# Expert weights of two mixtures: read from a DRAM table over the partitions instead of spread by a matmul

## What is computed

```python
def mixture0(x):                    # 1024 tokens, 16 experts, 4 of them chosen, in 2 of 4 groups
    scores = sigmoid(x @ router.T)
    tidx = topk(masked_by_group(scores + e_bias), 4)
    tw = scores[tidx] / (sum(scores[tidx]) + 1e-20) * 2.5
    h = silu(einsum('th,eih->tei', x, gate_w)) * einsum('th,eih->tei', x, up_w)      # i = 64
    yo = einsum('tei,ehi->teh', h, down_w)
    combine = zeros((T, 16)).at[token, tidx].add(tw)
    return einsum('te,teh->th', combine, yo) + shared_mlp(x)
# mixture3 is the same with 64 experts, 6 chosen in 4 of 8 groups, scores that include the bias,
# 1e-8 in the denominator and no factor 2.5
x = x + tanh(g_xattn[0]) * attention0(layernorm(x), ctx)
x = x + tanh(g_ffn[0]) * mixture0(layernorm(x))
...
x = x + tanh(g_ffn[3]) * mixture3(layernorm(x))
```

## Time and profile before

| | us |
|---|---|
| three plain runs | 698.71, 701.78, 708.68; median 701.78 |
| profiled execution | 699.08, of which the span is 697.3 |
| TensorE busy | 636.2 (91%) |
| VectorE busy | 419.7 (60%) |
| ScalarE busy | 377.8 (54%) |
| GpSimd busy | 195.4 (28%) |

### The profile page before, as it was taken

One profiled execution on the slowest core, in us unless ns is written; L12 is line 12 of the kernel. 1 busy time (PEld: TensorE's weight loads), 2 busy tenths in 40 slices (PEclk: granted clock), 3 DMA queues, 4 the chain that ended last, 5 costly groups with the idle time before them and its releaser, 6 DMA issues.

```text
span 697.3 us, 11157 instructions
## 1 busy us (share of the span) xinstructions
PE 636.2 (91%) x3615; PEld 440.7 (63%) x3618; DVE 419.7 (60%) x822; ACT 377.8 (54%) x663; POOL 195.4 (28%) x192
## 2 busy tenths in 40 slices
PE   6999987899699998999988999899996799999997
PEld 3457764675554446999953444467764577777885
DVE  2078839757732447777525565378839655656565
ACT  3567764455445334555554443577864356565553
POOL 4000024472010000000000244000023377777775
PEclk9999978999789999999999999999978999999999
DMA  8100002010000000000000000100001021121210
GB/s 298 44 1 3 1 1 76 1 47 0 1 0 1 0 1 0 1 1 0 1 1 0 24 23 16 46 2 1 2 17 60 1 61 51 55 49 56 60 31 31
DMA packets 9610, 18.55 MB, mean 27 GB/s; under 512 B 1856, under 2 KB 3024, under 8 KB 9440
## 3 DMA queue, kind: packets, MB, share of 16 engines
q1 hardware_dynamic: 9568, 18.01, 8.4%
HBM read 17.48 MB, written 0.52 MB: 26 GB/s over the span
## 4 chain that ended last, share of the span: by engine, by line
PE 79%; DVE 11%; ACT 5%; issue 3%; POOL 1%; DMA 1%; another core or an unknown queue 0%; DVEq 0%; ACTq 0%; SPq 0%; POOLq 0%
PE bank L676 7%; PE bank L678 7%; PE bank L677 7%; PE bank L593 4%; PE bank L926 4%; PE bank L913 4%; PE bank L604 4%; PE bank L485 3%; PE bank L619 3%; PE bank L522 2%; PE bank L690 2%; PE bank L534 2%; PE bank L1011 2%; PE bank L551 2%; PE bank L890 2%
## 5 line engine op out<-in xcount | busy, mean ns | idle before, releaser
L394 POOL TENSOR_TENSOR h_lo<-wc,h_hi 128x512 fp32r<-128x512 f32 x82 | 106.0, 1293 | 69.8 <-ACT h_hi L1200 68.6
L1609 DVE TENSOR_TENSOR wb<-wa,bank 128x512 f32<-128x512 f32 x80 | 55.0, 687 | 69.9 <-PE bank L678 64.3
L1192 ACT ACTIVATE wa<-bank 128x512 f32<-128x512 f32 x84 | 50.4, 600 | 75.5 <-PE bank L678 75.3
L1414 DVE TENSOR_REDUCE row_max<-bank 128x4 f32<-128x512 f32 (+1 forms) x96 | 65.7, 685 | 34.3 <-PE bank L593 19.4
L1127 ACT ACTIVATE wb<-wa 128x512 f32<-128x512 f32 x96 | 60.2, 629 | 33.7 <-DVE wa L1418 33.3
L676 PE MATMUL bank<-xn_hi,w_hi 128*128 128x512 f32 x168 | 68.8, 410 | 8.0 <-DVE wc L1613 3.7
L1418 DVE TENSOR_TENSOR wa<-bank,row_max 128x512 f32<-128x512 f32 x96 | 66.4, 691 | 9.9 <-ACT wb L1127 4.4
L1133 ACT ACTIVATE wc<-bank 128x512 f32<-128x512 f32 x96 | 57.0, 594 | 23.6 <-PE bank L551 15.2
L678 PE MATMUL bank<-xn_hi,w_lo 128*128 128x512 f32 x168 | 66.9, 398 | 0.0
L677 PE MATMUL bank<-xn_lo,w_hi 128*128 128x512 f32 x168 | 66.9, 398 | 0.0
L1200 ACT ACTIVATE h_hi<-wc 128x512 fp32r<-128x512 f32 x84 | 52.4, 624 | 16.1 <-DVE wc L1613 10.0
(11 more groups left out here) (271 smaller groups left out, 1260.4 us busy)
## 6 DMA issues: line engine op xcount, KB each, us to landing
ring<-in_experts SPq DMA_DIRECT2D x42, 256.0 KB, 2.6
ring<-in_experts SPq DMA_DIRECT2D x8, 192.0 KB, 2.4
mats<-in_mats SPq DMA_DIRECT2D x1, 1472.0 KB, 9.8
mats<-in_mats SPq DMA_DIRECT2D x1, 832.0 KB, 6.0
mats<-in_mats SPq DMA_DIRECT2D x2, 320.0 KB, 8.1
x<-in_x_t SPq DMA_DIRECT2D x1, 512.0 KB, 4.2
context<-in_ctx_t SPq DMA_DIRECT2D x1, 512.0 KB, 4.8
select<-in_select SPq DMA_DIRECT2D x1, 512.0 KB, 11.0
```

The source lines that it names most:

```text
L394: nc.gpsimd.tensor_tensor(h_lo[:, k % 2, :], wc[:, k % 2, :], h_hi[:, k % 2, :].bitcast(f32), ALU.subtract).then_inc(m_h_lo, 1)
L1414: v.tensor_reduce(row_max[:, u % 2, 0:heads], s, X, ALU.max).then_inc(a_max, 1)
L1609: v.tensor_tensor(wb[:, par, :], wa[:, par, :], bank[2 + par][:, :], ALU.mult)\
```

## The change

`split_weights`, the matmul `weight` and its semaphore `m_weight` are gone, and so is the use of the fourth 128 columns of each pair: loads and ScalarE's split cover 384 columns. `route_weights` writes the weights whole. After the transposition ScalarE copies only the 16 or 64 rows that carry experts. SyncE then (`half`) stores these rows of one half of the tokens to a table in DRAM, waits for the store, and for each of the four slots issues two loads (`pair_weights`), each of which reads one row of the table 64 times, into the upper or lower 64 partitions of `pair_w`, in the free region of `arena`. For later rounds the loads take all 1024 tokens at once, after the last `wc` that uses the slot, ahead of the load of the next pair's weights in the same queue. `wc` reads `pair_w` instead of a PSUM bank and waits for the slot's loads. The loop over rounds in SyncE's program is written out. Apart from the mixtures, VectorE fills 128 columns with ones at the start and TensorE multiplies them eleven times (`keep_busy`) before the first layer norm.

```diff
@@ -64,6 +64,7 @@
         q_rows = arena[:, 12288:16384].rearrange("p (g t) -> p g t", g=QUADS)
+        idle_w = arena[:, 512:512 + P]
...
@@ -106,7 +107,10 @@
         comb_pieces = sb("comb_pieces", [P, 8, P])
-        comb_t = sb("comb_t", [P, T], f32r)
+        comb_t = sb("comb_t", [P, T])
+        pair_w = arena[:, 8192:12288].rearrange("p (s t) -> p s t", s=4)
+        comb_rows = [nc.dram_tensor(f"comb_rows{n}", (e, T), f32).ap() for n, e in enumerate((16, 64))]
...
@@ -196,11 +200,13 @@
         m_shift = signal("m_shift")
-        m_g, m_u, m_cb, m_silu, m_t, m_h, m_h_hi, m_h_lo, m_down = (
-            signal(n) for n in ("m_gate", "m_up", "m_weight", "m_silu", "m_prod", "m_hidden", "m_hidden_hi",
+        m_g, m_u, m_silu, m_t, m_h, m_h_hi, m_h_lo, m_down = (
+            signal(n) for n in ("m_gate", "m_up", "m_silu", "m_prod", "m_hidden", "m_hidden_hi",
         m_x_lo = [signal("m_x_lo0"), signal("m_x_lo1")]
+        m_rows = signal("m_rows")
+        pair_in = [signal(f"pair_in{s}") for s in range(4)]
...
@@ -219,6 +225,8 @@
             m["q0"] = MOE[0]["pairs"] + 1 if n else 0
+            m["w0"] = 64 + 32 * (MOE[0]["rounds"] - 1) if n else 0
...
@@ -314,22 +322,46 @@
             def fill(m, q):
-                sp.dma_start(ring[:, (q + 3) % 4, :], m["weights"][q]).then_inc(w_in[(q + 3) % 4], 16)
+                sp.dma_start(ring[:, (q + 3) % 4, 0:384], m["weights"][q, :, 0:384]).then_inc(w_in[(q + 3) % 4], 16)
+            def pair_weights(m, q, slot, tokens):
+                for j in range(2):
+                    row = comb_rows[m["n"]][2 * q + j:2 * q + j + 1, tokens]
+                    sp.dma_start(pair_w[64 * j:64 * j + 64, slot, tokens],
+                                 row.to_broadcast([64, tokens.stop - tokens.start])).then_inc(pair_in[slot], 16)
-                with sp.Fori(1, m["rounds"]) as i:
-                    for j in range(4):
-                        slot = (j + 3) % 4
-                        sp.wait_ge(m_w_lo, m["q0"] + 4 * i + j - 3)
-                        sp.dma_start(ring[:, slot, :], m["weights"][ds(4 * i + j, 1), :, :].squeeze(0))\
-                            .then_inc(w_in[slot], 16)
-                sp.wait_ge(m_w_lo, m["q0"] + m["pairs"] - 3)
-                fill(m, m["pairs"])
+                n, u0, q0 = m["n"], m["u0"], m["q0"]
+                def refill(q):
+                    sp.wait_ge(m_w_lo, q0 + q - 3)
+                    fill(m, q)
+                def half(c):
+                    tokens = slice(c * HALF, c * HALF + HALF)
+                    sp.wait_ge(m_combE, 4 * n + c + 1)
+                    sp.dma_start(comb_rows[n][:, tokens], comb_t[0:m["E"], tokens]).then_inc(m_rows, 16)
+                    sp.wait_ge(m_rows, 16 * (2 * n + c + 1))
+                    for slot in range(4):
+                        pair_weights(m, slot, slot, tokens)
+                refill(4)
+                half(0)
+                refill(5)
+                refill(6)
+                half(1)
+                for i in range(1, m["rounds"]):
+                    last_use = FIRST_LAST_USE if i == 1 else LAST_USE
+                    for slot in range(4):
+                        sp.wait_ge(m_h, u0 + 2 + 8 * (i - 1) + last_use[slot] + 1)
+                        pair_weights(m, 4 * i + slot, slot, slice(0, T))
+                        if 4 * i + slot + 3 <= m["pairs"]:
+                            refill(4 * i + slot + 3)
...
@@ -465,6 +497,11 @@
+            def keep_busy(n, to):
+                for _ in range(n):
+                    mm(to[:, 0:P], idle_w, idle_w, start=True, stop=True)
...
@@ -685,11 +722,6 @@
-                def weight(slot, c, k):
-                    mm(bank[4 + k % 2][:, :], w_hi[:, slot, 384:512], comb_t[:, c * HALF:c * HALF + HALF],
-                       start=True, stop=True).then_inc(m_cb, 1)
...
@@ -698,8 +730,6 @@
                     pe.wait_ge(m_comb, 4 * n + c + 1)
-                    if c == 1:
-                        pe.wait_ge(m_h, u0 + 4)
...
@@ -714,8 +744,6 @@
                             combine_t(1)
-                            pe.wait_ge(m_combE, 4 * n + 2)
-                        weight(slot, c, k)
...
@@ -729,15 +757,14 @@
                 gate_up(*FIRST_ORDER[1], 1, u0 + 3, q0 + 1 + FIRST_ORDER[1][0], True)
-                pe.wait_ge(m_combE, 4 * n + 1)
-                for k in range(2):
-                    weight(*FIRST_ORDER[k], k)
-            pe.wait_ge(prepared, 3)
+            pe.wait_ge(prepared, 1)
+            keep_busy(11, bank[7])
+            pe.wait_ge(prepared, 4)
...
@@ -1177,7 +1204,7 @@
                         act.wait_ge(m_down, used)
-                    fn(w_hi[:, slot, :], ring[:, slot, :], ACT.Copy).then_inc(m_w_hi, 1)
+                    fn(w_hi[:, slot, 0:384], ring[:, slot, 0:384], ACT.Copy).then_inc(m_w_hi, 1)
...
@@ -1202,7 +1229,8 @@
                     act.wait_ge(m_combT, 4 * n + c + 1)
-                    fn(comb_t[:, c * HALF:c * HALF + HALF], bank[4 + c][:, :], ACT.Copy)\
+                    rows = slice(0, m["E"])
+                    fn(comb_t[rows, c * HALF:c * HALF + HALF], bank[4 + c][rows, :], ACT.Copy)\
...
@@ -1508,12 +1536,6 @@
                 return rt[:, n, 0:4 * e].rearrange("p (t e) -> p t e", t=4)
-            def split_weights(comb, e, c):
-                dst = comb_pieces[:, BH * c:BH * c + BH, :]
-                link(v.tensor_copy(dst[:, :, 0:e].bitcast(f32r), comb))
-                return v.tensor_tensor(dst[:, :, e:2 * e].bitcast(f32r), comb, dst[:, :, 0:e], ALU.subtract)
...
@@ -1591,15 +1613,18 @@
                 link(v.reciprocal(total, total))
-                link(v.tensor_tensor(picked, picked, total.unsqueeze(2).to_broadcast([P, 4, E]), ALU.mult))
+                share = total.unsqueeze(2).to_broadcast([P, 4, E])
+                pieces = comb_pieces[:, BH * c:BH * c + BH, 0:E]
                 if n == 0:
-                    link(v.tensor_scalar(picked, picked, 2.5, None, ALU.mult))
-                split_weights(picked, E, c).then_inc(m_comb, 1)
+                    link(v.tensor_tensor(picked, picked, share, ALU.mult))
+                    v.tensor_scalar(pieces, picked, 2.5, None, ALU.mult).then_inc(m_comb, 1)
+                else:
+                    v.tensor_tensor(pieces, picked, share, ALU.mult).then_inc(m_comb, 1)
-                def products(k, unit, weighed, older):
+                def products(k, unit, weighed, older, i=0):
...
@@ -1609,8 +1634,11 @@
                         dve.wait_ge(m_t, unit - 2 * n - 1)
-                        dve.wait_ge(m_cb, unit - 2 * n - 1)
-                        v.tensor_tensor(wc[:, par, :], wb[:, par, :], bank[4 + par][:, :], ALU.mult)\
+                        first = isinstance(i, int) and i == 0
+                        slot, c = (FIRST_ORDER if first else ORDER)[k]
+                        dve.wait_ge(pair_in[slot], m["w0"] + (32 * (c + 1) if first else 64 + 32 * i))
+                        v.tensor_tensor(wc[:, par, :], wb[:, par, :], pair_w[:, slot, c * HALF:c * HALF + HALF],
+                                        ALU.mult)\
...
@@ -1630,12 +1658,12 @@
                 route_weights(m, 1)
-                products(0, u0 + 4, True, True)
-                products(1, u0 + 5, True, True)
+                products(2, u0 + 4, True, True)
+                products(3, u0 + 5, True, True)
                     for k in range(4 if first else 0, 8):
-                        products(k, u0 + 2 + 8 * i + k, True, True)
+                        products(k, u0 + 2 + 8 * i + k, True, True, i)
...
@@ -1649,6 +1677,7 @@
+            v.memset(idle_w, 1.0).then_inc(prepared, 1)
...
@@ -1660,7 +1689,7 @@
             dve.wait_ge(a_bias, 1)
-            dve.wait_ge(prepared, 4)
+            dve.wait_ge(prepared, 5)
```

## The result

The changed kernel takes 718.56 us in the median (715.45 to 723.7, four runs) against 703.04 (four runs) beside it: a ratio of 1.022, 95% interval 1.012 to 1.033. It is slower, as forecast; whether by more than 2% these four runs leave open. The executions of a kernel fall into a quicker and a slower group, and ratios and intervals here are taken from the quicker one, medians from all. The profiled execution of the changed kernel took 715.45 us, with a span of 713.7 against 697.3.

The account below looks back on a forecast made before the run. TensorE bounds the mixtures' long middle (2.31 us a unit), waits the openings. From the profiled 699.1 us, +19.4 (loops), +7 (table) and -1 (warm-up) give 724.5, called 724; range 698 to 748.

Parts of the forecast that it names:

- The mechanism: Mixture loops: `wc`, now with two SBUF inputs, and GpSimd's instructions exclude each other; the second stands, then needs 0.55 or 1.17 us.
- Rival 1: Mixture loops: TensorE stays the bound, no engine stands, `wc` lasts 0.7 us; 688.5 us in all; chance 0.10.
- Rival 2: Mixture loops: VectorE and GpSimd pack well, 2.17 to 2.4 us a unit, 695 to 712 us; chance 0.17.
- rival 3: Mixture loops: GpSimd's queue goes ahead of a waiting `wc`, 2.7 to 3.06 us a unit, 733 to 759 us; chance 0.12.
- Rival 4: Mixtures' first rounds: the table is the cost, its loads landing near 8 us, 747 us in all; chance 0.04.
- loops of both mixtures, ends included: 72 units at 2.58 us instead of 2.31, the removed matmul included: +19.4 us.
- openings (table): Openings of both mixtures: the weights' way through DRAM delays the first `wc` of a half; +7 us, bounds +4 and +30.
- start: Before the first layer norm: eleven warm-up matmuls speed up the first four centring matmuls; -1 us, at best 1.9 gained.
- the simple cycle of 2.58: Mixture loops: GpSimd's `h_lo` always first, `wc` ends 0.55 us behind it; 2.58 us a unit, the pace taken.
- the walk that gave 2.52: Mixture loops: four units walked with `h_lo` and `w_lo`, a waiting VectorE served first; 10.1 us, 2.52 each.
- the 4.8 of the sum: Mixture openings: from ScalarE's copy to the first `wc`, store 2.0, issue 0.4 and load 2.4 us, together 4.8.
- The 1.6 us that I had added: Mixture openings: TensorE's clock falls while it waits; seven matmuls at twice their time, 1.6 us in both mixtures together.

Follow-up runs that it names:

- before_sbuf: Kernel before, with `wc` reading layer norm's output in SBUF instead of the PSUM bank, tenth matmul kept, no table, tokens' weights left out: 722.16 us, ratio 1.029.
- fix_psum: Changed kernel with the first product written in place into the up product's PSUM bank, where `wc` reads it: 695.96 us, ratio 0.991; measured again 693.85 us, 0.987.
- after_short_h: Changed kernel with GpSimd's `h_lo` cut from 512 to 64 tokens, the rest zeros filled once in each opening: 683.89 us in one run.
- no_table: Changed kernel without the table's store, loads and waits; `wc` multiplies by the layer norm's output in SBUF, tokens' weights left out: 711.29 us in one run.
- fix_short_w2: fix_psum with GpSimd's `w_lo` cut from 384 to 64 columns, the rest zeros filled once in each opening: 690.71 us in one run.
- fix_no_warm_b: fix_psum without the eleven matmuls at the start, measured beside fix_psum: 700.24 us, ratio 0.991 to the kernel before.

## Why the prediction was right, and where not

**The mechanism** was right, and it is shown: by before_sbuf (the operand alone makes the loss), fix_psum (moved back, the loss is gone with all else kept) and after_short_h (GpSimd's side shortened, gone as well). The Trainium skill ("SBUF — State Buffer", "Who interferes with whom") says that a VectorE instruction with two SBUF inputs contends with a GpSimd one that reads SBUF, that the shared access is an exclusive lock, and that the order of issue decides who blocks; the traces agree, with 0.54 us from GpSimd's end to VectorE's here, and 0.55 in the earlier trace rows.

**Rival 1** (TensorE stays the bound, 688.5) fell: it needed `wc` at 0.69 us. That it had a sound sum is seen in after_short_h, where `wc` is 0.70: 682.1. **Rival 2** (2.17 to 2.4 a unit) and **rival 3** (2.7 to 3.06) lie on either side of the 2.549. **Rival 4** had a load landing near 8 us; the 128 KB loads land in 3.0.

**The terms of the sum**, against the two profiled executions:

| term | forecast | measured |
|---|---|---|
| loops of both mixtures, ends included | +19.4 | +14.6 (12.5 + 0.8 + 0.7 + 0.6) |
| openings (table) | +7 | +6.7 (3.0 + 3.7) |
| start | -1 | -5.1 |
| stages between, behind | 0 | +0.2 |
| sum | +25.4 | +16.4 |

The loop was over-sized. I had 2.58 against 2.31, a difference of 0.27; measured were 2.549 against 2.337, that is 0.212. The step that failed is half in each. The 2.31 was the pace of the quiet middle alone, while behind the first round one unit takes 3.43 us in both kernels (560.03 to 563.46 before, 562.32 to 565.76 after): there TensorE waits for the next pair's `w_lo`, and the change adds nothing. And of the walks, the simple cycle of 2.58, in which GpSimd always comes first, is not what runs: 44 of 80 `wc` stood, and units alternate, as in the walk that gave 2.52, some with `wc` behind `h_lo` (1.69 us), some with `h_lo` behind `wc` (1.74). The measured pace lies between the two.

The openings came out near the forecast, 6.7 for 7. ScalarE's copies of the weights' rows in the changed kernel:

```profile
112.22 0.59 ACT L1233 ACTIVATE comb_t<-bank 16x512 f32<-16x512 f32 x1 [2.71 <-PE bank L734]
...
125.42 0.59 ACT L1233 ACTIVATE comb_t<-bank 16x512 f32<-16x512 f32 x1 [1.28 <-PE bank L734]
...
534.81 0.59 ACT L1233 ACTIVATE comb_t<-bank 64x512 f32<-64x512 f32 x1 [3.52 <-PE bank L734]
...
549.18 0.59 ACT L1233 ACTIVATE comb_t<-bank 64x512 f32<-64x512 f32 x1 [1.76 <-PE bank L734]
```

From the end of a copy to the `wc` that waits for it pass 5.3, 5.3, 5.7 and 6.2 us, not the 4.8 of the sum. Against that, the first copy of each mixture ends 0.5 and 0.8 us earlier behind the first gate matmul than before, not 0.2 and 0.3. So the first `wc` comes 2.4 and 2.5 us later there (forecast 2.2 and 2.0), and the fifth, the first of the second half, 3.7 and 3.0 (forecast 3.2 and 2.0): the second half of mixture 2 was not hidden, VectorE waits 2.93 us for its loads. The granted clock up to the fifth `wc` is 0.87 in mixture 1 where it was 0.94, and 0.85 in mixture 2 where it was 0.83. The 1.6 us that I had added for it are about what the waits were short by. Without any weights to wait for (no_table) the fifth `wc` of mixture 2 comes 27.6 us behind the first gate matmul, against 30.9 before and 33.9 with the table: about half of the wait in the changed kernel was there before.

The start was under-sized: I bounded it by the four matmuls of the earlier trace rows, which are 1.7 us shorter but over only 1.4 us earlier, since the eleven are not "over well before" x lands but end 0.5 us behind it; and the profiles have 2 to 5 us there. Since the forecast was 724 and the profiled execution 715.45, these two terms are the whole miss of some 9 us: 4.8 from the loop, 4.1 from the start.

Of the signs I had named, TensorE "about 80% busy" needs a word: the page shows 90%, because matmul records overlap the wait of the next one; counted by issue, 350 times 0.231 in 99.70 us, it is 81%.

## What to carry over

Before an operand moves from PSUM to SBUF, write down for that instruction and for all that run beside it on the other engine where every operand lies, and look in the trace for a pair of the new kind: the two such rows gave the loops' loss to within 5 us, where the removed matmul alone promised a gain of 16.6. If the place must change, keep the other operand in PSUM; here one product written in place turned 2% slower into 1% faster. A transfer that replaces a matmul early in a stage is paid in latency: here the openings grew by 6.7 us, with four waits of 2.0 to 3.5 us in them. The steps that it relieves are worth counting as carefully as the ones it adds.

## What the runs showed of the hardware that I had not expected

**The table's way in the changed kernel.** SyncE's rows at the opening of mixture 2 (start, us, queue, line):

```profile
535.42 0.47 SPq L348 DMA_DIRECT2D comb_rows<-comb_t  x1
537.68 4.94 SPq L334 DMA_DIRECT2D arena<-comb_rows  x8
```

The store is waited for 2.26 us from its issue. Each of the eight loads, which spread one row over 64 partitions, takes 0.6 us to issue, not the 0.42 of the earlier trace rows, so the last pair's load is issued some 4.9 us behind the store's landing. The weights' own loads land in 3.9 us instead of 2.4, and no wait for them is among the changed kernel's waits in the mixtures.

**`w_lo` as the second.** Behind a `wc` of 0.69 us it takes another 0.89 us (after_short_h), where `h_lo` needs 1.12 to 1.15 more and `wc` 0.54: most of the own work of each still lies ahead when the other ends.

**The clock of a stage that no edit touches.** The stages between the mixtures take 357.8 to 363.0 us in eight profiled executions, but 368.5 to 371.1 in four (fix_short_w2, before_sbuf, fix_no_warm_b and fix_psum_b). The last is the same kernel as fix_psum, and its profiled execution, 704.32 us, was the longest of its six. The two from 440 to 480 us, first fix_psum, then fix_psum_b (us, busy us of PE, PEld, DVE, ACT, POOL with counts, granted clock, DMA share, GB/s):

```profile
440.00:450.00 10.00, 8.88 (x45) 4.69 (x46) 2.70 (x6) 3.50 (x6) 0.00 (x0) 0.84 0.00 0
450.00:460.00 10.00, 8.61 (x96) 5.53 (x96) 7.52 (x13) 7.95 (x15) 0.00 (x0) 1.00 0.01 2
460.00:470.00 10.00, 9.94 (x127) 7.07 (x126) 7.25 (x14) 7.69 (x16) 0.45 (x1) 1.00 0.01 2
470.00:480.00 10.00, 9.81 (x127) 7.04 (x125) 8.52 (x16) 7.13 (x16) 0.45 (x1) 1.00 0.01 2
```

```profile
440.00:450.00 10.00, 8.03 (x32) 4.54 (x31) 3.21 (x7) 4.96 (x8) 0.00 (x0) 0.76 0.04 13
450.00:460.00 10.00, 8.03 (x44) 3.66 (x42) 3.27 (x5) 5.00 (x8) 0.00 (x0) 0.90 0.00 0
460.00:470.00 10.00, 9.76 (x84) 6.55 (x84) 7.23 (x11) 5.49 (x11) 0.00 (x0) 0.62 0.01 2
470.00:480.00 10.00, 10.00 (x99) 7.28 (x97) 5.21 (x10) 5.71 (x14) 0.45 (x1) 0.70 0.01 2
```

In the second TensorE is as busy in the last two stretches, but its clock is a mix of the two levels, 1.2 and 2.4 GHz (0.62 and 0.70 of full in the mean), and it issues 84 and 99 matmuls where the first has 127 at full clock. Ahead of the fall it had been busy 8.03 of 10 us twice; in the other execution 8.88 and 8.61, and there the clock came to 1.00 and stayed. What decides between them within one and the same kernel stays open. With 10.9 us between these two executions it is two thirds of the 16.4 us that were asked for, and it is why every comparison above goes by stage.
